# One pool of eight PSUM banks in a fused two-layer attention and FFN kernel on one Trainium2 core

## The reference, cut to what matters

```
x = x + attn_a(layernorm(x))   # 16 heads of 16; window |i-j| <= 32 and 4 global tokens; softmax; biases
x = x + ffn(layernorm(x))      # h = silu(x Wg) * (x Wu), 768 wide; y = h Wd; int weights / 127
x = x + attn_b(layernorm(x))   # num = exp(rope(q) rope(k) s); den = sum(exp(q k s)); causal after the division
x = x + ffn(layernorm(x))      # the same weights again
```

## The kernel before, in words

| step | engine | what it does | line |
|---|---|---|---|
| `X` | PE | transposes the normed x into two banks | L1031 |
| `T`, `V`, `O`, `W` | PE | Q/K projection, V projection, output projection, pair swap for the rotation | L1087, L1008, L1021, L1095 |
| `G`, `U`, `FD` | PE | gate, up and down products of the FFN | L1057, L1057, L1075 |
| `A1`, `A2`, `AV` | PE | scores of A for the maxima, scores again for the exponentials, values | L818/L826, same, L925 to L939 |
| `DP`, `NP`, `BV` | PE | a pair of denominator units, a pair of numerator units, values of B | L952, L973, L988 |
| `DE`, `NE`, `A2E` | ACT | exponentials of a pair | L1173, L1163, L1156 |
| `XH`, `T1`, `GT`, `AH` | ACT | high half of x, of Q/K; tanh of the gate; first half of A's values | L1191, L1212/L1221, L1202, L1186 |
| `X1`, `T2`, `H`, `I`, `AT`, `BT`, `OX`, `E`, `AM` | DVE | the last readers of the banks of `X`, `T`, `G`, `U`, `AV`, `BV`, `O`, `FD`, `A1` | L1453, L1489/L1495, L1460, L1466, L1378, L1384, L1408, L1482, L1347 |

## Time and profile before

### The profile page before, as it was taken

One profiled execution on the slowest core, in us unless ns is written; L12 is line 12 of the kernel. 1 busy time (PEld: TensorE's weight loads), 2 busy tenths in 40 slices (PEclk: granted clock), 3 DMA queues, 4 the chain that ended last, 5 costly groups with the idle time before them and its releaser, 6 DMA issues.

```text
span 2151.9 us, 63371 instructions
## 1 busy us (share of the span) xinstructions
PE 1816.0 (84%) x25221; PEld 1124.9 (52%) x25221; DVE 1429.2 (66%) x2978; ACT 1440.0 (67%) x3591; POOL 793.8 (37%) x1140
## 2 busy tenths in 40 slices
PE   5577889889898988989898898989898898988785
PEld 3353545555564555556465555646455554645344
DVE  5373768677676867667676766768676776855634
ACT  2227676676867677686767768686776868676590
POOL 0523243433434343342434344243334334243431
PEclk9697999999999999999999999999999999998887
DMA  5213344242434434243433424253343424342221
GB/s 149 74 40 92 78 115 106 79 111 84 110 74 121 97 84 108 83 111 69 128 90 86 113 80 109 68 131 87 107 99 90 106 79 123 70 105 81 72 67 36
DMA packets 129205, 199.51 MB, mean 93 GB/s; under 512 B 26721, under 2 KB 60513, under 8 KB 128881
## 3 DMA queue, kind: packets, MB, share of 16 engines
q1 hardware_dynamic: 128912, 195.44, 35.9%
HBM read 67.87 MB, written 51.52 MB: 55 GB/s over the span
## 4 chain that ended last, share of the span: by engine, by line
PE 43%; ACT 23%; DVE 16%; issue 6%; POOL 5%; SPq 3%; DMA 2%; ACTq 0%; POOLq 0%; DVEq 0%
PE gu_bank L1057 12%; ACT s_bank L1173 8%; PE gu_bank L1087 5%; PE d_bank L1075 4%; ACT probs_B L1163 4%; ACT probs_A L1156 3%; POOL tmp L1601 3%; DVE top L1347 3%; PE s_bank L952 3%; PE s_bank L988 2%; PE gu_bank L1021 2%; PE gu_bank L1031 2%; SPq L579 2%; PE s_bank L939 2%; PE s_bank L973 2%
## 5 line engine op out<-in xcount | busy, mean ns | idle before, releaser
L1173 ACT ACTIVATE s_bank<-s_bank 128x512 f32<-128x512 f32 x1024 | 604.4, 595 | 114.8 <-PE s_bank L952 114.7
L1596 POOL TENSOR_TENSOR h<-tmp,h 128x512 f16<-128x512 f32 x192 | 227.8, 1186 | 435.4 <-DVE h L1477 435.4
L1163 ACT ACTIVATE probs_B<-s_bank 128x512 f32<-128x512 f32 x640 | 335.1, 613 | 44.9 <-PE s_bank L973 42.6
L1057 PE MATMUL gu_bank<-xT,w_g 128*128 128x256 f16 x1536 | 204.4, 277 | 33.7 <-DVE tmp L1460 30.0
L1202 ACT ACTIVATE tmp<-gu_bank 128x512 f32<-128x512 f32 x192 | 115.6, 602 | 164.1 <-PE gu_bank L1057 155.8
L1057 PE MATMUL gu_bank<-xT,w_u 128*128 128x256 f16 x1536 | 211.3, 279 | 10.7 <-DVE src_a L1489 4.1
L952 PE MATMUL s_bank<-pack_b 48*128 48x512 f16 x1024 | 181.9, 393 | 42.6 <-DVE o_raw L1378 21.9
L1613 POOL TENSOR_SCALAR_AFFINE_SELECT probs_B<-probs_B 128x256 f32<-128x256 f32 x512 | 192.7, 412 | 44.8 <-ACT probs_B L1163 44.6
L1460 DVE SCALAR_TENSOR_TENSOR tmp<-tmp,gu_bank 128x512 f32<-128x512 f32 x192 | 130.7, 681 | 114.9 <-ACT tmp L1202 114.7
L1075 PE MATMUL d_bank<-w_d,h 128*128 128x256 bf16 x1536 | 199.9, 273 | 5.5 <-POOL h L1596 4.2
L1173 ACT ACTIVATION_READ_ACCUMULATOR s_bank<-s_bank 128x1 f32 x1024 | 200.4, 196 | 0.0
(11 more groups left out here) (162 smaller groups left out, 3192.1 us busy)
## 6 DMA issues: line engine op xcount, KB each, us to landing
pack_b<-src_b SPq DMA_DIRECT2D x768, 64.0 KB, 2.4
pack_a<-src_a SPq DMA_DIRECT2D x384, 64.0 KB, 2.3
x<-in_L_attn_a_x_dram SPq DMA_DIRECT2D x32, 512.0 KB, 4.4
o_scr_A<-o_raw SPq DMA_DIRECT2D x64, 256.0 KB, 2.3
o_scr_B<-o_raw SPq DMA_DIRECT2D x64, 256.0 KB, 2.5
xn<-o_scr_A SPq DMA_DIRECT2D x32, 256.0 KB
rden_on<-r_scr_A SPq DMA_DIRECT2D x32, 256.0 KB
x_scr<-x SPq DMA_DIRECT2D x16, 512.0 KB, 2.9
```

The costliest lines, as they stand in the source:

```text
L1057: last = pe.matmul(bank[:, f * D:(f + 1) * D], w_part[:, k, c:c + P], given[:, k, half * D:(half + 1) * D], start=k == 0 and part == 0 and ...
L1163: act.activation(probs["B"][:, i, :], score_bank("NP", n // 2, q, n % 2)[:, :], ACT.Exp, scale=SM_SCALE / W_SCALE ** 2)\
L1173: act.activation(bank[:, :], bank[:, :], ACT.Exp, scale=SM_SCALE / W_SCALE ** 2, accum_out=den[:, 0, j, 2 * tile + e, t:t + 1]).then_inc(d ...
L1596: pool.tensor_tensor(h[1][:, i % 2, :], tmp[:, i % 2, :], h[0][:, i % 2, :], ALU.subtract)\
```

## The change

All eight banks become one list `psum`. Which bank a use gets is worked out before the kernel is built, by `bank_places`: it walks `STEPS`; at each use it takes, among the banks whose last holder's reader can have been fed by then (`OWED`), the one whose last reader has the smallest place. `bank_free` then waits for exactly the reader of the use that held that bank before. `gu_taken` counts as it did; the number that a wait asks for is now counted over the readers (`TOOK`).

```diff
-BANKS = 5
-TAKEN = {"A1": 2, "TM": 1, "A2": 2, "AV": 2, "DP": 2, "DT": 1, "NP": 2, "BV": 1}
+BANKS = 8
 USES = {"X": KT, "T": 1, "V": 1, "O": 1, "W": 1, "G": 1, "U": 1}
+TAKERS = {"X": "X1", "T": "T2", "V": "VC", "O": "OX", "W": "W1", "G": "H", "U": "I"}
+SCORES = {"A1": "AM", "TM": "TC", "A2": "A2E", "AV": "AT", "DP": "DE", "DT": "BR", "NP": "NE", "BV": "BT"}
+HELD = {"A1": 2, "TM": 1, "A2": 2, "AV": 2, "DP": 2, "DT": 1, "NP": 2, "BV": 1, **USES}
...
+def bank_places():
+
+    found, held, until, need = {}, [None] * BANKS, [-1.0 - b for b in range(BANKS)], [-1.0] * BANKS
+    for place, kind, n, block, q in STEPS:
+        for key in holders(kind, n, block, q):
+            b = min(range(BANKS), key=lambda b: (need[b] >= place, until[b]))
+            found[key] = b, held[b]
+            held[b], until[b], need[b] = key, PLACE[leaves(*key)], OWED[leaves(*key)]
     return found
...
-        s_bank = [ctx.enter_context(nc.psum_tensor(f"s_bank{i}", [P, S], F32)) for i in range(BANKS)]
-        gu_bank = [ctx.enter_context(nc.psum_tensor(f"gu_bank{i}", [P, S], F32)) for i in range(2)]
-        d_bank = ctx.enter_context(nc.psum_tensor("d_bank", [P, S], F32))
+        psum = [ctx.enter_context(nc.psum_tensor(f"psum{i}", [P, S], F32)) for i in range(BANKS)]
...
+            def bank_free(*key):
+
+                before = BANK_OF[key][1]
+                if before is None:
+                    return
+                kind, n, block, r, e = before
...
+                elif kind == "FD":
+                    pe.wait_ge(d_taken, 2 * FN[block, r] + n + 1)
+                else:
+                    pe.wait_ge(gu_taken, taken(kind, n, block, r, e))
...
             def gu(kind, n, block, q, k=0):
 
-                use = gu_use(kind, n, block, q, k)
-                if use > 1:
-                    pe.wait_ge(gu_taken, use - 1)
-                return gu_bank[use % 2]
+                bank_free(kind, n, block, q, k)
+                return bank_of(kind, n, block, q, k)
```

The table of places is new in every line (`START` and the shift of 425 stay), for example:

```diff
-    "BV": (1132, 1253, 1325, 1443),
+    "BV": (1144.5, 1282.4, 1356, 1456.7),
```

More of the change, by code:

```diff
@@ new lines @@
+    "PBT2": (1020.8, 1024.9, 1028.9, 1033),
+    "OAOR": (748.4,),
+    "OAOL": (744.5, 746.4),
+    "OAOM": (786.6, 789.1),
+    "OAOH": (814.4, 820.3),
+    "OAOW": (815.9, 821.8),
+    "OAO": (830, 848.6),
+    "OAOX": (835.5, 854.1),
+    "OBOR": (1445.8,),
+    "OBOL": (1449.6, 1481.1),
+    "OBOM": (1468.2, 1491.1),
+    "OBOH": (1471.2, 1494.1),
+    "OBOW": (1477.3, 1495.6),
+    "OBO": (1500.7, 1511),
+    "OBOX": (1510, 1516.4),
+    "F2L0": (1518.8,),
+    "F2L1": (1523.3,),
+    "F2L2": (1529.5,),
@@ new lines @@
+    "F2L3": (1530.2,),
+    "F2L4": (1531,),
+    "F2L5": (1531.7,),
+    "F1L0": (856.4,),
+    "F1L1": (860.9,),
+    "F1L2": (874.3,),
+    "F1L3": (880.6,),
+    "F1L4": (881.4,),
+    "F1L5": (882.1,),
+    "PBL0": (991.8,),
+    "PBL1": (996.3,),
+    "PBL2": (1003.2,),
+    "PBL3": (1003.9,),
+    "PBL4": (1004.7,),
+    "PBL5": (1005.4,),
+    "NAL0": (260.7,),
+    "NAL1": (265.2,),
+    "NAL2": (281,),
+    "NAL3": (281.7,),
+    "NAL4": (282.5,),
+    "NAL5": (283.2,),
+    "PAX": (312.5,),
@@ L271, in ahead @@
         count += k in kinds and n == 0
-def ring_places():
-    found, first, held = {}, 0, {}
-    for _, kind, n, block, q in STEPS:
-        if kind in TAKEN:
-            here = []
-            for e in range(TAKEN[kind]):
-                bank = (first + e) % BANKS
-                here.append((bank, held.get(bank)))
-                held[bank] = kind, n, q, e
-            first += TAKEN[kind]
-            found[kind, n, q] = here
-    return found
-RINGS = ring_places()
+TOOK = numbered({TAKERS[kind]: uses for kind, uses in USES.items()})
@@ new lines, with holders @@
+PLACE = {(kind, n, block, q): place for place, kind, n, block, q in STEPS}
+def holders(kind, n, block, q):
+    if kind == "FD":
+        return [("FD", n // (FT // 2), block, q, 0)] if n % (FT // 2) == 0 else []
+    if kind == "U" and n == 0:
+        return []
+    held = [(kind, n, block, q, e) for e in range(HELD.get(kind, 0))]
+    return held + [("U", 0, block, q, 0)] * (kind == "G" and n == 0)
+FED_BY = {"A2E": "A2", "DE": "DP", "NE": "NP", "XH": "X", "GT": "G", "T1": "T", "TC": "TM", "AH": "AV", "AM": "A1", "AT": "AV",
+          "BT": "BV", "BR": "DT", "X1": "X", "T2": "T", "VC": "V", "OX": "O", "W1": "W", "H": "G", "I": "U", "E": "FD"}
@@ new lines, with owed @@
+ON_ACT, AFTER_ACT = ("A2E", "DE", "NE", "XH", "GT", "T1", "TC", "AH"), {"AT": "AH", "X1": "XH", "T2": "T1", "H": "GT"}
+def owed():
+    found, most = {}, [-1.0, -1.0]
+    for _, kind, n, block, q in STEPS:
+        if kind not in FED_BY:
+            continue
+        dve, step = int(kind not in ON_ACT), (n, block, q)
+        if kind == "E":
+            need = PLACE["FD", n * (FT // 2) + FT // 2 - 1, block, q]
+        else:
+            need = PLACE[(FED_BY[kind],) + step]
+        if kind in AFTER_ACT:
+            need = max(need, found[(AFTER_ACT[kind],) + step])
+        most[dve] = max(most[dve], need)
+        found[(kind,) + step] = most[dve]
+    return found
@@ new lines, with leaves @@
+OWED = owed()
+def leaves(kind, n, block, q, e):
+    if kind == "FD":
+        return "E", n, block, q
+    if kind == "AV" and e:
+        return "AH", n, block, q
+    return {**SCORES, **TAKERS}[kind], n, block, q
+def bank_places():
[5 more added lines that the diff above has]
+            held[b], until[b], need[b] = key, PLACE[leaves(*key)], OWED[leaves(*key)]
+    return found
@@ L292, in tile_jobs @@
+BANK_OF = bank_places()
 def tile_jobs(kinds):
@@ L512, in build @@
         st_uT = st2[:, KT * HID:2 * KT * HID].rearrange("p (k n) -> p k n", k=KT)
-        all_banks = [b[:, :] for b in s_bank] + [b[:, :] for b in gu_bank] + [d_bank[:, :]]
+        all_banks = [b[:, :] for b in psum]
         NC, NSPLIT, NBANKS = 14, 4, 15
@@ L794, in split_passes @@
+            def pair_free(kind, n, q):
+                block = "B" if kind in ("DP", "DT", "NP", "BV") else "A"
+                for e in range(HELD[kind]):
+                    bank_free(kind, n, block, q, e)
             def split_passes(lhs, rhs):
```

269 lines of the change are left out of this document (115 added, 154 removed), and 70 rows, old and new, of the table AT.

## The result

The changed kernel takes **2088.3 us** in the median of 4 runs (2086.04 to 2093.75), the kernel before 2158.65 on the same chip (2154.69 to 2162.85). The ratio is 0.9678, interval 0.9647 to 0.9708: 70 us or 3.2% faster. Forecast were 2106 us and a range of 2065 to 2146. So the sign, the range and the size hold, and the gain came out larger than the 55 us of the sum.

The account below looks back on a forecast made before the run. No single bound: PE, then ACT, then chains between engines pace each 123.03 us turn. Bank waits kept 0.8 + 0 + 0 + 1.0 + 2.1 = 3.9 us, x 14 = 55 us: 2106 us, range 2065 to 2146.

Parts of the forecast that it names:

- the thirteen: PE's stops for PSUM banks in one turn, 12.05 us in sum, all forecast to go to first order.
- 1, `T` 2 of `PB`: Q/K projections of `PB`: the 0.80 us stop at `T` 2 goes, 0.8 us per turn kept.
- 2 and 3 without `W`: Stops before `X` of `PB` and at the first `DP`: PE then waits for layer norm or pack, 0 kept.
- 4, five stops under ACT: Five stops, 5.07 us, where ACT is nearly full: 1.0 us per turn kept, between 0.3 and 1.3.
- 5, `G` 5, `U` 3, `T` 3: Stops behind the full ACT, where ACT and DVE wait for PE: 2.1 us per turn kept.
- the number of turns: Factor of 14 turns' worth, from numerator pairs' 35.0 us behind `AT` over 2.5 per turn, filling and draining included.
- two rivals, one of either sign: Clock returns: up to 42 us more gain, 2064, chance 0.05; or clock is lost: 2192, chance 0.05.
- slower, by the clock: Longer stops before the two layer norms cost clock, 3.0 us in each of 14 turns: 2192 us, chance 0.05.
- Nearly all gained: ACT stretch less tight than its busy share: 8.3 x 14 = 116 us gained, 2045 us, chance 0.10.
- No difference: Stops only move to data: less than 0.8 us per turn kept, about 2155 us, chance 0.07.

Follow-up runs that it names:

- w_ends: Changed kernel with all old reader waits back only while the pipeline fills and drains; 2107.09 us, ratio 0.98 to the kernel before.
- w_pb: Changed kernel where the `T` steps of `PB` and the four `W` also wait for their old readers; 2103.41 us, ratio 0.979 to the kernel before.
- w_act: Changed kernel where `AV` 2, `AV` 3, `NP` 1, `NP` 4 and `G` 1 of `F2` also wait for their old readers; 2107.53 us.
- w_g5: Changed kernel where `G` 5 and `U` 3 of `F2` and `T` 3 of `PA` also wait for their old readers; 2124.65 us.
- filler: Changed kernel plus dummy matmuls, three ahead of `X` of `PB` and `F2`, five ahead of a sequence's first `DP`, denominator pair's waits swapped; 2064.06 us.
- filler_np: Kernel with dummy matmuls ahead of `X` and the first `DP`, plus five more ahead of the first numerator pair; 2062.48 us.

## Why the prediction was right

**Sign and mechanism.** The bank waits went as the comparison of old and new holders had said: of the thirteen only 0.26 us at `AV` 0 is left in the turn shown, and the turn went from 123.03 to 119.96 (forecast: near 119). `NP` no longer waits for `AT`; `X` and `DP` wait for data, longer than before; ACT stays as full in its stretch, 37.10 of 40.0 us against 37.92.

**Term by term,** in us per turn; measured is the restored or removed part alone, first from the medians over 14 turns (the ends are in it), then from the 13 turns of the profile:

| point | predicted | by the medians | by the turns |
|---|---|---|---|
| 1, `T` 2 of `PB` (run with the other `T` and with `W`, whose 0.72 is in point 3) | 0.8 | 1.2 | 1.2 |
| 2 and 3 without `W`: `AV` 0, `NP` 18, first `DP` | 0 | not run alone | |
| 4, five stops under ACT | 1.0 | 1.5 | 1.3 |
| 5, `G` 5, `U` 3, `T` 3 | 2.1 | 2.7 | 3.3 (in the longest of four executions) |
| clock | 0 | −1.6 | −1.0 |
| all | 3.9 | | 3.6 |

Each term was right in kind. Each came out above its forecast, point 5 most, but the 12 us of a difference are 0.9 us per turn, so none of the three is shown to be too low by itself. The sum had no term for the clock, and the clock took something back. The two errors have opposite signs, so that the turn came out so near (3.9 and 3.6) is in part luck. New stops were missed as well, the longest of them at `DP` 6. It takes a bank whose reader is `DE` 4, and waits 0.62 us for it in the turn shown (timeline of the kernel after; the second row is the rest at `AV` 0):

```profile
1626.98 0.39 PE L1017 MATMUL psum<-pack_b 48*128 48x512 f16 x2 [0.62 <-ACT psum L1236]
...
1715.38 0.38 PE L990 MATMUL psum<-probs_gq,v_aug_A 128*17 128x4 f32 x32 [0.26 <-ACT probs_A L1219]
```

The old and new holders had been compared at the old times, and a PE that comes earlier finds readers late that were early enough before.

**The term that was mis-sized is the number of turns.** The sum took 14 turns' worth, from the numerator pairs' 35.0 us, so one turn's worth, 3.9 us, for filling and draining together. They gave 8.1 + 12.9 = 21.0 in the profiles, and 20.2 in w_ends. The 14 was counted from one kind of wait, and that kind hardly occurs in the ends (numerator pairs of the kernel before, between its first and its fourteenth `DT`):

```profile
L973 PE MATMUL s_bank<-pack_b 48*128 48x256 f16 (+3 forms) x834 | 95.3, 302 | 56.9 <-DVE o_raw L1378 31.4 <-ACT s_bank L1173 17.9 <-DVE o_raw L1384 4.5
```

Of the 35.0 us behind `AT`, 31.4 lie in the 13 turns and 3.6 in the ends. But the ends are 278.63 + 259.05 = 537.68 us long, which is 4.4 turns, and 21.0 over 4.4 is 4.8 us for each turn's length, not far above the 3.6 of the middle. So what failed in the sum is that it took the ends for one turn. Why they hold somewhat more than their length was not tried; that fewer sequences are under way there, so that less can hide a wait of PE, is a guess. 3.6 x 13 + 21.0 = 67.8 is the whole difference of the spans.

**The clock.** The prediction had nothing in its sum for it and weighed two rivals, one of either sign. The rival "slower, by the clock" had the mechanism right: longer stops in front of data, and half clock behind them. It had the place partly wrong, for one of the two is behind the first `DP`, where I had argued from one stop of 1.58 us that nothing happens. The length of that one stop does not settle it: in another turn of the kernel after, the first `DP` waited only 1.12 us, and the clock behind it fell all the same (timeline and window of the kernel after):

```profile
287.46 0.39 PE L1017 MATMUL psum<-pack_b 48*128 48x512 f16 x2 [1.12 <-DMA pack_b<-src_b]
...
289.00:292.30 3.30, 3.30 (x16) 1.82 (x15) 1.98 (x4) 2.53 (x7) 2.56 (x3) 0.50 0.63 182
```

What else must come together for the clock to fall is open. And the rival had the size wrong: 1.0 to 1.6 us per turn, not 3.0. The 3.0 could have been seen to be too much: a clock of 0.72 over 6 us is 1.7 us of lost clock, the most that it can have added to the turn of 126.03 us if the rest of it ran at 1.00. Since 3.6 are kept beside it, it decided nothing here. The Trainium skill's rule on cycling through PSUM (TensorE: Matmul & The Clock Gate, section A second HAM failure mode: psum-queue depth-cycling) would have had the change give clock back. The trace disagrees: with most of the short stops between banks gone, the granted clock of the middle fell from 0.99 to 0.97, and with two of them put back, in w_pb, it rose a little.

"Nearly all gained" fell by ACT, as argued: w_act shows that 5.07 us of stops are worth about 1.5. "No difference" fell by w_g5.

**Two readings were off and changed nothing.** Of the five stops that the prediction puts in the window from 1540 to 1557.5, three lie in it and two in the next, which also had 1.00. And its list of stops is not complete: PE also waited 0.54 us before `T` 0 of `PB`, for data, and 0.34 us at `NP` 7 for `BT` (timeline of the kernel before):

```profile
1525.00 1.25 PE L1087 MATMUL gu_bank<-xT,wb_qk 128*128 128x512 f16 x5 [0.54 <-DVE xT L1453]
...
1571.23 0.64 PE L973 MATMUL s_bank<-pack_b 48*128 48x384 f16 x8 [0.34 <-DVE o_raw L1384]
```

## What to carry to other kernels

When an in-order engine waits for buffers, read each stop's place before you count it: here 2.09 us of stops behind which other engines wait were worth all of their length, 5.07 us beside a full engine about a third of it. Scale by the length of the run and not by counting one kind of wait: filling and draining held 21 of the 68 us. A static choice of buffers needs honest times of the readers, not just an order: the same rule on the same eight banks gave 3% less or 16% more time by its table. When short stops are merged into long ones in front of data, look at the granted clock, and try work without use in the gap: here it gave back about 20 us.

## What was not expected of the hardware

- Dummy matmuls (five took 1.25 us) made the kernel faster, by about 20 us. PE sat idle for 0.83 us instead of 2.09 ahead of the first `DP` in the turn shown, and the granted clock behind it was 1.00 instead of 0.72. How much work in the gap is needed was not tried.
- A clock that rises need not pay: from filler to filler_np the mean went from 0.958 to 0.967, the time by 2 us, which is within the intervals.
